# Sixteen subtractions and twelve rounding steps of a fused transformer block move from VectorE to GpSimd

## The reference

```python
x = x + _L0_xattn_ref(_layernorm(x), ctx)      # first stage
x = x + _L0_ffn_ref(_layernorm(x), gate_w, up_w, down_w, gate_s, up_s, down_s)   # first stage
x = x + _L1_xattn_ref(_layernorm(x), ctx, mask)
x = x + _L1_ffn_ref(_layernorm(x), w_gate, w_up, w_down)

def _L0_xattn_ref(x, weight):          # a matmul of fp8-rounded operands
    xq = quant_dequant_act_1x128(x)            # absmax of each 1 x 128 block, round to e4m3
    wq = quant_dequant_weight_128x128(weight)  # absmax of each 128 x 128 block, round to e4m3
    return jnp.einsum('emk,enk->emn', xq, wq)
```

## Time and profile before

| | us |
|---|---|
| median of 3 runs | 705.13 (704.87 to 706.69) |
| the profiled execution's own time | 709.98 |
| its span, first to last instruction | 708.0 |
| busy in the span: PE, DVE, ACT, POOL | 642.6, 584.5, 470.0, 363.6 |
| first group starts on PE (first chunk) | 39.76 |
| last group starts on PE | 289.39 |
| mean granted TensorE clock | 0.992 |

### The profile page before, as it was taken

How to read it: one execution, slowest core, us unless ns; L and a number is a source line. 1 busy time by engine, 2 the same in 40 slices (tenths; PEclk the granted TensorE clock), 3 DMA queues, 4 the chain that set the end, 5 groups by cost and what they waited for, 6 DMA issues and landing times.

```text
span 708.0 us, 12360 instructions
## 1 busy us (share of the span) xinstructions
PE 642.6 (91%) x4055; PEld 376.8 (53%) x4086; DVE 584.5 (83%) x1331; ACT 470.0 (66%) x965; POOL 363.6 (51%) x277
## 2 busy tenths in 40 slices
PE   1689799999999999997979999899999999999986
PEld 0266466757675666763434444354555555555543
DVE  6889899999999888357759894679899998999775
ACT  3747467766776655377758761466888788887834
POOL 2022131323222314057646751019999999999970
PEclk9999999999999999999999999999999999999999
DMA  8981223333331332708999971144468765667411
GB/s 208 237 287 23 78 79 103 95 102 93 87 103 33 104 76 68 250 11 199 261 166 343 222 192 38 31 88 92 91 120 133 133 136 104 132 125 140 108 46 45
DMA packets 173130, 88.21 MB, mean 125 GB/s; under 512 B 150546, under 2 KB 152594, under 8 KB 172052
## 3 DMA queue, kind: packets, MB, share of 16 engines
q1 hardware_dynamic: 167188, 71.94, 44.8%
q10 hardware_dynamic: 3408, 11.27, 5.0%
q0 software_dynamic: 2480, 4.33, 3.5%
HBM read 51.20 MB, written 4.19 MB: 78 GB/s over the span
## 4 chain that ended last, share of the span: by engine, by line
PE 55%; DVE 23%; issue 7%; ACT 7%; DMA 6%; POOL 2%; SPq 0%; DVEq 0%; ACTq 0%
PE ps L1892 13%; PE ps L1739 7%; PE ps L1964 7%; PE ps L1834 7%; PE ps L1816 6%; DMA arena<-arena 5%; PE ps L1754 4%; PE ps L1872 3%; PE ps L1932 3%; DVE X L1148 3%; DVE arena L1239 2%; PE ps L1691 2%; DVE arena L1081 1%; PE ps L1665 1%; PE ps L1941 1%
## 5 line engine op out<-in xcount | busy, mean ns | idle before, releaser
L1739 PE MATMUL ps<-arena 128*128 128x256 f16 x1408 | 160.1, 273 | 10.3 <-DVE arena L1239 6.7
L1739 PEld LDWEIGHTS ps<-arena 128*128 128x128 f16 x1408 | 135.6, 98 | 36.0 <-DVE arena L1239 10.4
L488 POOL TENSOR_TENSOR arena<-arena 128x256 f16<-128x256 f32 x88 | 57.7, 675 | 181.6 <-ACT arena L663 181.2
L1892 PE MATMUL ps<-arena 128*128 128x512 bf16 x486 | 115.4, 379 | 6.8 <-ACT arena L877 2.9
L560 POOL TENSOR_TENSOR arena<-arena 128x1024 f32<-128x1024 f32 x44 | 104.0, 2363 | 21.8 <-DVE arena L1536 17.3
L561 POOL TENSOR_TENSOR arena<-arena 128x1024 f32<-128x1024 f32 x44 | 103.9, 2362 | 0.0
L1754 PE MATMUL ps<-arena 128*128 128x512 f16 x352 | 80.1, 384 | 3.6 <-POOL arena L488 3.5
L1892 PEld LDWEIGHTS ps<-arena 128*128 128x128 bf16 x512 | 49.1, 98 | 60.0 <-DVE arena L1528 3.5
L656 ACT ACTIVATE arena<-ps,gs 128x256 f32<-128x256 f32 x88 | 40.7, 466 | 51.8 <-PE ps L1739 51.7
L1834 PE MATMUL ps<-arena 128*128 128x512 f16 x256 | 59.4, 387 | 4.7 <-issue 3.6
L1964 PE MATMUL ps<-arena 128*128 128x512 bf16 x251 | 59.1, 379 | 2.3 <-ACT arena L955 1.8
(11 more groups left out here) (167 smaller groups left out, 1200.8 us busy)
## 6 DMA issues: line engine op xcount, KB each, us to landing
arena<-in_ctx_t SPq DMA_DIRECT2D x7, 1024.0 KB, 6.1
arena<-in_wg_t SPq DMA_DIRECT2D x16, 256.0 KB, 3.8
arena<-in_wu_t SPq DMA_DIRECT2D x16, 256.0 KB, 4.4
arena<-in_wd_t SPq DMA_DIRECT2D x16, 256.0 KB, 5.0
arena<-in_ctx_n SPq DMA_DIRECT2D x4, 1024.0 KB, 10.8
arena<-in_wu_t ACTq DMA_DIRECT2D x4, 1024.0 KB, 5.6
arena<-in_wd_t ACTq DMA_DIRECT2D x4, 1024.0 KB, 6.0
out_x<-X SPq DMA_DIRECT2D x16, 256.0 KB, 2.3
```

Of the source, the lines that this page charges most:

```text
L488: nc.gpsimd.tensor_tensor(hl[:, c, at:at + 2 * P], b_h[n % 4], hh[:, c, at:at + 2 * P], ALU.subtract).then_inc(b_hl_r, 1)
L1739: last = M(bank(n % 2)[:, 2 * P * i:2 * P * i + 2 * P], W[:, b, c * P:c * P + P], part[:, b, at:at + 2 * P], start=(b == 0 and part is xhT ...
L1892: last = M(bank(2 * (n % 2) + i), d_qT[u][:, b, :], W[:, b, D * n:D * n + D], start=(b == 0), stop=(b == KD - 1))
```

## The change

DVE no longer makes low parts of the context, nor the rounding additions and subtractions of batches 1 to 3; POOL does both, with the same operands, in new places of its list. The grids stay on DVE. The high parts of batch 0 move on ACT from group 0 into the prelude, and their low parts to POOL's prelude. In group 0 ACT's order changes behind chunk 8, and DVE's grids and hidden values stand in another order. PE's and SP's lists are the same as before.

```diff
+            def context_low(e, b):
+                pool.wait_ge(c_hi_r, KD * e + b + 1)
+                nc.gpsimd.tensor_tensor(context_part(e, b, 1), wdq[:, e % 2, b, :], context_part(e, b, 0), ALU.subtract).then_inc(c_lo_r, 1)
+
+            def context_rounding(e, b):
+                w, grid = wdq[:, e % 2, b, :], ctxT[:, e % 2, b, :]
+                pool.wait_ge(c_grid, 8 * e + 2 * b + 2)
+                nc.gpsimd.tensor_tensor(w, w, grid, ALU.add).then_inc(c_round, 1)
+                pool.wait_ge(c_round, rounds_by(e, b) - 1)
+                nc.gpsimd.tensor_tensor(w, w, grid, ALU.subtract).then_inc(c_round, 1)
...
             root("a", 1, 1)
+            context_low(0, 0)
             root("a", 2, 0)
             root("b", 0, 0)
+            context_low(0, 1)
+            context_low(0, 2)
             root("b", 1, 1)
+            context_low(0, 3)
 
...
+                more, odd, e, n0, n1 = g + 1 < PAIRS, g % 2 == 1, (g + 2) // 2, 2 * g + 2, 2 * g + 3
+                ahead = not odd and 0 < g and e < B
+                if g == 1:
+                    context_rounding(1, 2)
+                    context_rounding(1, 3)
+                if ahead:
+                    context_rounding(e, 0)
                 h_low(g, 0)
                 if more:
                     root("a", n1, 1)
+                if g in (3, 5):
+                    context_low(e, 3)
                 h_low(g, 1)
+                if g == 1:
+                    context_low(1, 2)
                 h_low(g, 2)
                 h_low(g, 3)
+                if g == 1:
+                    context_low(1, 3)
+                if ahead:
+                    context_rounding(e, 1)
                 h_low(g, 4)
                 h_low(g, 5)
+                if g == 0:
+                    context_rounding(1, 0)
+                if ahead:
+                    context_rounding(e, 2)
                 if more:
                     root("b", n0, 0)
                 h_low(g, 6)
                 h_low(g, 7)
+                if ahead:
+                    context_low(e, 0)
                 h_low(g, 8)
                 h_low(g, 9)
                 if more:
                     root("b", n1, 1)
                 h_low(g, 10)
+                if g == 0:
+                    context_low(1, 0)
+                    context_rounding(1, 1)
                 if n0 + 2 < NT:
                     root("a", n0 + 2, 0)
+                if ahead:
+                    context_rounding(e, 3)
+                    context_low(e, 1)
+                    context_low(e, 2)
+                if g == 0:
+                    context_low(1, 1)
 
             for g in range(PAIRS):
                 b_group(g)
...
                 b_silu(g, 8)
+                if g == 0:
+                    b_silu(g, 9)
                 if more:
                     b_normal(n0)
-                if not odd and e < B and g:
+                if ahead:
                     context_back(e, 1)
                     context_high(e, 1)
-                if g == 0:
-                    context_back(1, 0)
-                    context_high(1, 0)
-                b_silu(g, 9)
+                if g:
+                    b_silu(g, 9)
                 if not more:
                     mask_copy(3)
                 b_silu(g, 10)
...
                 b_high(g, 10)
                 if g == 0:
-                    context_back(1, 1)
-                    context_high(1, 1)
+                    context_scaled(1, 3)
+                    context_back(1, 0)
+                    context_high(1, 0)
                 if more:
                     b_normal(n1)
...
+                if g == 0:
+                    context_back(1, 1)
+                    context_high(1, 1)
...
             a_evac(0)
             context_back(0, 2)
             context_back(0, 3)
+            context_high(0, 0)
             a_back(1)
+            context_high(0, 1)
             a_evac(1)
             act.wait_ge(ds_ps, 1)
             nc.scalar.activation(ds_bc[:, :], bank(7), ACT.Copy).then_inc(ds_r, 1)
+            context_high(0, 2)
+            context_high(0, 3)
             a_scale(2)
...
 
             def b_group(g):
                 more, odd, e, following, n0, n1 = g + 1 < PAIRS, g % 2 == 1, (g + 2) // 2, (g + 3) // 2, 2 * g + 2, 2 * g + 3
-                if g == 1:
-                    context_rounding(1, 2)
-                if not odd and e < B and g:
+                ahead = not odd and e < B and g
+                if ahead:
                     context_grid(e, 0)
                 if more:
                     a_grids(n0)
-                if not odd and e < B and g:
-                    context_rounding(e, 0)
+                if ahead:
                     context_grid(e, 1)
-                if g == 1:
-                    context_rounding(1, 3)
                 if not more:
                     weight_scales()
                 if g:
                     b_down(2 * g - 1)
-                if g == 0:
-                    context_low(0, 0)
                 b_hidden(g, 0)
...
-                if g == 0:
-                    context_low(0, 1)
-                if not odd and e < B and g:
+                if ahead:
                     context_grid(e, 2)
-                if g in (3, 5):
-                    context_low(e, 3)
-                if g == 1:
-                    context_low(1, 2)
-                if g == 0:
-                    context_low(0, 2)
-                    context_low(0, 3)
                 if more:
                     a_normal(n1)
-                if not odd and e < B and g:
-                    context_rounding(e, 1)
                 if g == 0:
                     context_top(1)
                 b_hidden(g, 3)
-                if g == 1:
-                    context_low(1, 3)
...
+                    a_parts(n1, 1)
+                if g == 0:
+                    b_hidden(g, 9)
+                if more:
+                    b_low(n0)
                 if g == 0:
                     context_grid(1, 1)
-                if more:
-                    a_parts(n1, 1)
-                if not odd and e < B and g:
...
+                    b_hidden(g, 9)
                 if more:
                     b_stats(n1)
                 b_hidden(g, 10)
-                if g == 0:
-                    context_low(1, 0)
                 if n0 + 2 < NT:
                     a_stats(n0 + 2)
                 if g == 0:
-                    context_rounding(1, 1)
                     dve.wait_ge(ds_r, 1)
-                if not odd and e < B and g:
-                    context_low(e, 1)
+                    context_grid(1, 2)
...
                 if g == 0:
                     context_grid(1, 3)
-                    context_low(1, 1)
-                if not odd and e < B and g:
-                    context_rounding(e, 3)
                 if more:
                     b_down(2 * g)
-                if not odd and e < B and g:
-                    context_low(e, 2)
```

More of the change, by code:

```diff
@@ L677, in b_group @@
                     context_high(1, 2)
-                if g == 0:
-                    context_high(0, 1)
                 if g in (3, 5):
@@ L682, in b_group @@
                     context_high(e, 3)
-                if g == 0:
-                    context_high(0, 2)
                 b_silu(g, 1)
@@ L691, in b_group @@
                 b_silu(g, 3)
-                if g == 0:
-                    context_high(0, 3)
                 if sums[g] < sums[g + 1]:
@@ L1324, in b_group @@
                 b_hidden(g, 7)
-                if not odd and e < B and g:
+                if ahead:
                     context_grid(e, 3)
-                if g == 0:
-                    context_rounding(1, 0)
                 if odd and following < B:
@@ L1338, in b_group @@
                     b_center(n0)
+                    a_parts(n1, 1)
[3 more added lines that the diff above has]
+                    b_low(n0)
                 if g == 0:
                     context_grid(1, 1)
-                if more:
-                    a_parts(n1, 1)
-                if not odd and e < B and g:
-                    context_low(e, 0)
-                if more:
-                    b_low(n0)
-                if not odd and e < B and g:
-                    context_rounding(e, 2)
-                if g == 0:
-                    context_grid(1, 2)
-                b_hidden(g, 9)
+                if g:
+                    b_hidden(g, 9)
                 if more:
```

13 lines of the change are left out of this document (2 added, 11 removed).

## The result

The changed kernel takes 729.35 us (median of 4 runs, 725.49 to 731.46) where the kernel before, run beside it, takes 705.0 us: ratio 1.0328, 95% interval 1.0298 to 1.0357. The direction was forecast, the size was not: +24.3 us instead of +4.3, and outside the range.

What follows compares the result with a forecast made beforehand. The stage was taken as bound by PE, with waits of 0.5 to 1.6 us on top. Groups 0 and 1 +3.5 us plus groups 2 and 4 +0.8 gave +4.3, from 705.13 to 709.4 us; range 701 to 714.

Steps and rivals of the forecast that it cites:

- the term for groups 0 and 1 together: End of group 1: +3.5 us, including +0.5 us at its start from group 0; bounds +1.5 and +5.5.
- the root of tile 4: End of group 0: root delayed behind POOL's low part and rounding, to 75.5 us from 73.42; group 1 starts +0.5 us.
- The group 1 term: Group 1: chunk 5 waits for POOL's last low part, +4.4 us; after DVE catches up, +3.5 us with group 0's part.
- groups 2 and 4 term: Groups 2 and 4: DVE relief against instructions held by POOL, +0.4 us each, +0.8 for both; bounds -3.2 and +4.0.
- +0.9: Groups 2 and 4, ahead of the first hidden value: POOL's first rounding pair holds DVE, +0.9 us.
- +1.1: Groups 2 and 4: POOL's second rounding pair runs against the grids ahead of a later hidden value, +1.1 us.
- -1.6: Groups 2 and 4: waits at the places of 146.70 and 152.62 us go as DVE sheds work, -1.6 us.
- groups 3 and 5 at nothing: Groups 3 and 5: one low part each moves to POOL, in time for its product, 0 us.
- the prelude at nothing: Prelude: high parts fit ACT's idle gaps and low parts POOL's, 0 us; up to 1.3 us later if ACT's were too short.
- The average holding: Each instruction moved to POOL gives back between 0 and 1.15 us of DVE time; 0.45 us taken on average.
- POOL holds DVE every time: Rival: in groups 2 and 4 eleven moved instructions hold DVE, +4.9 us each; +13.3 us total, 718.4 us; chance 0.07.
- The expected gain: Groups 0 to 5: DVE sheds 16 low parts and 24 additions and subtractions, 28.5 us, by itself neither gain nor loss.

Runs made afterwards that it cites:

- e4: Changed kernel with POOL taking the root of tile 4 ahead of low part (1,0) and rounding (1,1): 722.11 us, ratio 1.0215 to the kernel before.
- e5: e4 with low parts (1,2) and (1,3) ahead of the `h_low` of chunk 1 in POOL's list: 714.72 us, ratio 1.0127 to the kernel before.
- e2: Changed kernel with all low parts back on DVE, the twelve roundings staying on POOL: 713.47 us, ratio 1.0142 to the kernel before.
- e3: Kernel before with only batch 0's high parts in ACT's prelude and its low parts in POOL's prelude: 708.71 us, ratio 1.0015.
- e9: e5 with roundings back on DVE and batch 0's low parts on POOL behind tile 1's low part: 708.06 us, ratio 1.0023 to the kernel before.
- e10: Kernel before with batch 0's high parts in ACT's prelude and its low parts on POOL behind tile 1's low part: 707.98 us, ratio 1.0009.
- e7: Kernel before with 16 unneeded POOL subtractions on a spare tile at the rounding places of groups 2 and 4: 712.98 us, ratio 1.0111.
- e8: e7 with a memset of the spare tile in place of each subtraction: 708.04 us, ratio 1.0018 to the kernel before.

## Why the prediction was right and wrong

The forecast was 20.0 us too low. 4.7 of them lie in the term for groups 0 and 1 together (1.2 of these come from the prelude), 7.4 in groups 2 and 4, 3.3 in groups 3 and 5, and 4.7 outside the stage, without a cause that was found.

- **Right: the direction and what bounds the kernel.** PE waits for late preparations, and work shed from DVE is worth only what it does to those waits.
- **Right: the root of tile 4.** Forecast were the root at 75.5 us, `b_low` at 77.6 and PE idle for 5 us and more. The root ended at 77.55, `b_low` began at 79.36 and PE stood for 6.16 us; 1.2 us of the lateness is the prelude's delay. Group 1 started 1.6 us late (+0.5 forecast, bound +2.0), and e4 shows that 3.8 us of the wait are nothing but the place of one POOL entry in its list.
- **The group 1 term: place right, size wrong.** Forecast was a stall at chunk 5 with +3.5 us by the group's end; it was +8.2 us. The low parts cost what was worked out: from the first matmul of `a_product` to chunk 5 PE took 6.52 us (94.40 to 100.92) instead of 2.57 (91.01 to 93.58), +3.95 us where the sum has 3.9. Two other pieces were mis-sized. `a_product` began 3.4 us late, not 0.5: 1.6 us at the group's start and 1.75 in the chunks ahead of it, of which e4 leaves about 0.3 to the clock. And chunk 5 ran at the lower clock behind the waits, 3.62 us instead of 1.91, for which the sum had nothing (no run has these waits without the lower clock behind them, so the 1.7 us is read from the rows). Behind it PE caught up 0.9 us, as forecast. e5 took the stall and this stretch of lower clock away, and the group came back to 36.8 us.
- **Wrong: the groups 2 and 4 term.** +0.4 us each was the sum of +0.9, +1.1 and -1.6. The first two are right: the waits for the two hidden values grew from 0.32 us and the 0.54 of the earlier trace rows to 1.01 and 1.57. **The -1.6 is the step that failed.** The tail was to lose its waits, since DVE has less to do there. It grew by 2.0 us. I had placed the first two pairs of roundings against DVE's list and not the fourth pair and the low parts behind it: right behind the root, beside the normalization, the scale arithmetic and `b_low` of the next group's first product, with no slack in between (3.69 us for 1.82, which is nearly all of the 2.0). In e2, which has the fourth pair there but no low part, the same way takes 2.92 us, so the pair is 1.1 us of it and the low part with it 0.8. It cost 2 x 3.7 us against the sum.
- **Wrong: groups 3 and 5 at nothing.** +1.7 us each, all of it clock: 80 matmuls in 10.56 us instead of 8.89.
- **Wrong: the prelude at nothing.** +1.2 us, at its bound but for another reason. I had looked for ScalarE's gaps; e3, e9 and e10 show that it is POOL that holds DVE's small instructions.
- **The average holding was not what failed.** I took 0.45 us for each moved instruction. Summed over the stage, DVE's instructions ran 26.4 us over the medians that their kinds have in the kernel before, against 6.3 there: 20.1 us for 40, 0.50 each. So the rival "POOL holds DVE every time" is not what happened, though its 718.4 us came nearest. What matters is which instruction is held, not how much.
- **The expected gain** of 28.5 us of DVE work is worth nothing by itself. e2 sheds 5.5 us of it in group 2 and loses 3.8 us, e7 sheds none and loses 3.6.

The rule that the prediction took from the Trainium skill ("SBUF — State Buffer") goes further than I used it: besides two-input instructions the pair is taken by `cast` and `tensor_scalar` in their two-port modes, never by `tensor_reduce`, and a GpSimd instruction that only writes does not meet a two-input one. The traces agree: CAST 1.18 us instead of 0.22, `TENSOR_SCALAR` 128x4 0.98 instead of 0.20, `TENSOR_REDUCE` 2.28 beside two subtractions, and the two-input instruction of e8 at 0.67. The rows of before could have warned: there the 128x4 `TENSOR_SCALAR` L1115 already takes 0.50 us instead of 0.20 in five groups, each time beside an `h_low` of POOL.

**What stays open.** The stage explains 19.7 us; the medians differ by 24.3. The profiled execution of before was itself 4.85 us over its median, and its part behind the stage took 418.5 us, that of the changed one 416.6 and that of e7 414.4. Those parts run the same instructions, so the rest may come from the clock or from how executions differ; no run settled which. In the ten experiments the difference of the medians lies between 1.3 us under and 2.3 us over what group 7 is late (e2 without its one long run 1.6 under), so 4.7 us is more than any of them shows. That the 1.7 us of groups 3 and 5 come only with both halves of the change, and with the low parts late in group 1, is seen in the traces of single executions, after and e4; why the clock falls at one pause of 2.00 us and not at another was not found.

## What to carry to other kernels

Before work is moved from DVE to GpSimd, lay it beside DVE's list instruction by instruction: what reads PSUM, reduces or takes statistics runs on, what casts, scales or has two SBUF inputs stands until GpSimd is done, and that costs most where a chain of small instructions leads to the next product. In a list served in order, a short instruction that others wait for (here a root of 0.55 us) goes ahead of the long ones that nobody needs yet. And price the low clock that can follow a pause of TensorE, but only where TensorE itself then sets the pace: 1.7 us at chunk 5 of group 1 and in each of groups 3 and 5, but about 0.3 us at the head of group 1, where it would have waited for others anyway.

## What the runs showed of the hardware

- A DVE `TENSOR_SCALAR` on a 128x4 tile is held as long as one on 128x512: 0.98 us instead of 0.20, to the end of POOL's instruction. One on 128x1 (L1081, 0.15 us) was not lengthened in 12 meetings of the changed kernel, nor was `RECIPROCAL` on 128x4 in 8 (0.18 us).
- DVE's `TENSOR_REDUCE` and `BATCH_NORM_STATS2`, and `SCALAR_TENSOR_TENSOR` with a PSUM operand, were not lengthened beside POOL's instructions in groups 2 to 4 of e7 (5, 6 and 18 meetings).
- A stretch of the lower clock can cost nothing: with it 24 matmuls of group 0 take 6.85 us (before), without it 5.35 (e7), and the group is 41.2 us long in both, since PE then waits 1.56 or 3.06 us for the next one.
- The clock behind equal pauses was not the same: 2.00 us of idle time ahead of group 3, 10.56 us in e4 and 8.89 us in e5 for the same 80 matmuls, with only group 1 edited between them.
- POOL's subtraction of 128x512 took 1.04 us with all operands in one tile (e7), 1.15 with a half-width output, and 1.26 us for the rounding's f32 ones.
